# Context rows padded to 128, evidence blocks in one DMA each, weights in parts, and new orders around the guests of a four-layer attention kernel

## The reference

```python
def cross(xq, ctx):                       # layers 0, 2, 3; k, v of 1500 rows
    q, (k, v) = heads(xq @ Wq + bq), heads2(ctx @ Wkv + bkv)
    return softmax(q @ k.T / sqrt(8)) @ v
# layer 0
x = x + cross(ada(x), ada(ctx_1024)) @ Wp + bp
# layer 1, one head of 128
nx = layer_norm(x)
evidence = softmax((nx @ Wq) @ (ctx_1024 @ Wk).T / sqrt(128)) @ (ctx_1024 @ Wv)
c = concat(nx, evidence, cond)
routed = sum_e softmax(c @ router_W)[e] * (silu(c @ e_w1[e] + b1) @ e_w2[e] + b2)
x = x + sigmoid(silu(c @ gate_w1) @ gate_w2) * (routed @ out_w + out_b)
# layers 2 and 3
x = x + gate_a * self_attention(modulate(ln(x)))
x = x + cross(ln(x), ctx_1024)
x = x + gate_m * (gelu(modulate(ln(x)) @ W1 + b1) @ W2 + b2)
```

## Time and profile before

| | |
|---|---|
| median of 3 runs | 873.31 us (870.72 to 874.67) |
| the profiled execution | 873.29 us, its span 871.5 us |
| mean granted TensorE clock | 0.955 |
| busy: TensorE, VectorE, ScalarE, GpSimd | 780.7, 580.4, 514.1, 386.8 us |
| DMA | 106.55 MB, mean 122 GB/s |
| chain that ended last | TensorE 74%, DMA 9%, VectorE 6% |

### The profile page before, as it was taken

The page is one execution under the profiler, slowest core; times in us unless marked ns, Lnnn a source line. Parts: engine busy times, 40 slices in busy tenths (PEclk is TensorE's granted clock), DMA queues, the critical chain, the costliest instruction groups (busy, mean ns, idle before and its releaser), DMA issues.

```text
span 871.5 us, 23503 instructions
## 1 busy us (share of the span) xinstructions
PE 780.7 (90%) x9735; PEld 548.0 (63%) x9735; DVE 580.4 (67%) x1344; ACT 514.1 (59%) x826; POOL 386.8 (44%) x540
## 2 busy tenths in 40 slices
PE   6659999997699899967889999899999989999986
PEld 4227667765466576546657776666667666666664
DVE  7945778673288477722873777766778847777824
ACT  8435767665155567642654778565766646777552
POOL 8754767753017277620261775525332514333000
PEclk9797999999799999989996999999999989999999
DMA  8695545835614246443250553441643423543100
GB/s 216 174 245 146 151 132 171 236 92 168 168 28 127 74 108 170 131 143 110 84 155 13 144 140 90 127 127 52 174 131 98 142 74 104 162 131 101 37 3 11
DMA packets 87230, 106.55 MB, mean 122 GB/s; under 512 B 13278, under 2 KB 79838, under 8 KB 86868
## 3 DMA queue, kind: packets, MB, share of 16 engines
q1 hardware_dynamic: 83092, 103.04, 42.9%
q10 hardware_dynamic: 4032, 2.00, 0.9%
HBM read 41.17 MB, written 0.23 MB: 48 GB/s over the span
## 4 chain that ended last, share of the span: by engine, by line
PE 74%; DMA 9%; DVE 6%; ACT 4%; POOL 4%; issue 2%; SPq 1%; POOLq 0%; ACTq 0%
PE oacc_ps L692 14%; PE ring_ps L667 14%; PE score_ps L681 12%; PE ring_ps L644 7%; PE ring_ps L651 7%; DMA tok<-ctx_nat 6%; DVE max_sb L785 3%; PE ring_ps L636 2%; PE ring_ps L1042 2%; PE ring_ps L1596 2%; DMA kstack<-part_sb 2%; PE ring_ps L657 1%; POOL kstack L2103 1%; ACT prob_sb L764 1%; PE ring_ps L1072 1%
## 5 line engine op out<-in xcount | busy, mean ns | idle before, releaser
L785 DVE TENSOR_REDUCE max_sb<-ring_ps 128x1 f32<-128x500 f32 x576 | 368.8, 673 | 122.2 <-PE ring_ps L667 120.3
L764 ACT ACTIVATE prob_sb<-score_ps 125x896 f32<-125x896 f32 x288 | 256.6, 922 | 93.8 <-PE score_ps L681 91.1
L860 POOL TENSOR_TENSOR key_sb<-key_sb,part_sb 128x500 f32<-128x500 f32 x72 | 82.4, 1144 | 318.7 <-ACT key_sb L746 318.4
L667 PE MATMUL ring_ps<-kstack,qstack 128*128 128x500 bf16 x576 | 200.0, 386 | 18.5 <-DMA kstack<-part_sb 11.8
L681 PEld LDWEIGHTS score_ps<-qstack,kstack 128*128 128x128 bf16 (+1 forms) x2304 | 141.9, 103 | 39.6 <-issue 10.8
L681 PE MATMUL score_ps<-qstack,kstack 128*128 128x112 bf16 (+1 forms) x2304 | 160.3, 216 | 1.8 <-ACT prob_sb L764 1.0
L692 PE MATMUL oacc_ps<-prob_sb,val_sb 125*32 125x168 f32 (+1 forms) x3456 | 141.6, 297 | 0.5 <-ACT prob_sb L764 0.5
L692 PEld LDWEIGHTS oacc_ps<-prob_sb,val_sb 125*32 125x32 f32 x3456 | 98.4, 110 | 49.2 <-issue 21.9
L667 PEld LDWEIGHTS ring_ps<-kstack,qstack 128*128 128x128 bf16 x576 | 52.1, 99 | 79.5 <-issue 28.4
L865 POOL TENSOR_TENSOR part_sb<-key_sb,part_sb 128x500 bf16<-128x500 f32 x72 | 82.2, 1142 | 5.1
L851 POOL TENSOR_SCALAR hat_sb<-nat_sb,norm_now 125x128 f32<-125x128 f32 x184 | 80.3, 453 | 1.4
(11 more groups left out here) (266 smaller groups left out, 984.2 us busy)
## 6 DMA issues: line engine op xcount, KB each, us to landing
kstack<-part_sb SPq DMA_DIRECT2D x432, 125.0 KB, 2.4
nat_sb<-ctx_nat SPq DMA_DIRECT2D x16, 672.0 KB
qstack<-qpart_sb SPq DMA_DIRECT2D x60, 112.0 KB, 2.3
nat_sb<-ctx_T SPq DMA_DIRECT2D x8, 750.0 KB, 4.7
ev_in<-ctx_T SPq DMA_DIRECT2D x16, 250.0 KB
ev_in<-ctx_nat SPq DMA_DIRECT2D x16, 250.0 KB
w_sb<-ctx_nat SPq DMA_DIRECT2D x5, 672.0 KB
w_sb<-weights SPq DMA_DIRECT2D x1, 3076.5 KB, 10.9
```

The lines of the kernel that those rows point to most:

```text
L667: last = pe.matmul(ps[:, 0:KB], queries(p, n, D), kstack[:, u, p, j * KB:(j + 1) * KB], start=True, stop=True)
L764: return act.activation(dst, score_ps[0:CK, c % 2, :, 0:HALF], ACT.Exp)
L785: return dve.tensor_reduce(max_sb[:, p, j:j + 1], ring_ps[:, self.bank[f"{i}.{name}"], 0:KB], AX.X, ALU.max)
L860: return pool.tensor_tensor(rest, rest, part_sb[:, 0, cols], ALU.subtract)
```

## The change

1. `ctx_nat` is padded to 128 rows, and a context comes in one DMA (it was 112 rows and 13 rows).
2. A new array `ctx_blocks` holds the evidence blocks as 128 rows x 2 x 512, one DMA each.
3. The weights of layers 1 and 2 come in four parts, one at the start of each of the periods 0 to 3, each behind a count of finished statistics. The modulation weights move from the startup to period 1. Contexts 5, 6 and 7 are loaded for their statistics at the starts of periods 0, 1 and 2, context 4 behind item 0's keys; its statistics move from VectorE's startup to period 0.
4. Only the first half batch's queries are stacked ahead of item 0's keys; the other six DMAs go behind them.
5. The second half of `kstack` is cleared behind item 0's hats and gets its ones behind item 0's values.
6. TensorE: V0 to V2 of period -1 stand ahead of MTa, K2 behind MTb; period 0 begins with S0 and S1.
7. mods goes from period 0, anch from period 3, to period 4 behind S9.
8. The tables are written anew. e0a's and e0b's heads run further in periods 4 and 8 (w, l, g2, o0 to o2 at their ends); e2b's own scores go from period 18 to the end of 17; e3a's proj goes from period 22 to 20 and its u0 and u1 from 24 to 23. A table LATE gives periods 7 and 11 an order of their own on TensorE and VectorE, in which the maxima (of items 8 and 12) stand further behind the scores.

```diff
-            sp.dma_start(to[0:NAT_SPLIT, :, :], ctx_nat[n, 0:NAT_SPLIT]).then_inc(loaded, 16)
-            sp.dma_start(to[NAT_SPLIT:CK, :, :], ctx_nat[n, NAT_SPLIT:CK]).then_inc(loaded, 16)
+            sp.dma_start(to, ctx_nat[n]).then_inc(loaded, 16)
...
+                order = LATE[eng, p].split() if (eng, p) in LATE else order
+                if eng == "pe" and p == 0:
+                    order = ["S0", "S1", *[n for n in order if n not in ("S0", "S1")]]
...
-                    for t in range(2):
-                        n = HB * self.h + 2 * k + t
-                        if kind == 0:
-                            sp.dma_start(block[:, t, 0:KB], ctx_T[n][:, i * KB:(i + 1) * KB]).then_inc(into, 16)
-                        else:
-                            sp.dma_start(block[0:CK, t, :].rearrange("p (c k) -> p c k", c=4), ctx_nat[n][:, 4 * i:4 * i + 4, :])\
-                                .then_inc(into, 16)
+                    sp.dma_start(block, ctx_blocks[2 * self.h + k, NJ * kind + i]).then_inc(into, 16)
...
-            stack_queries(sp, queries_ready(d0), a0.qstacked, (0, 1))
+            stack_queries(sp, queries_ready(d0), a0.qstacked, (0, 1), (0,))
             sp.wait_ge(keys_cleared, 1)
...
-            for n in range(STATS_FIRST, 7):
-                load_context(sp, stats_buffer(n), n, stats_loaded[n])
-            w0, w1 = W_AT["L2_W_mod"][0], W_AT["L1_Wq"][0]
-            sp.dma_start(w_sb[:, w0:w1], weights[:, w0:w1]).then_inc(loaded_wm, 16)
-            sp.wait_ge(stats_done, STATS_AT[2] + 1)
-            load_context(sp, stats_buffer(7), 7, stats_loaded[7])
+            stack_queries(sp, queries_ready(d0), later_queries, halves=(1,))
+            load_context(sp, stats_buffer(4), 4, stats_loaded[4])
             sp.wait_ge(keys_cleared, 2)
-            for p in a0.periods(-1):
+            a0.run("sp", sp, -1)
+            for p in a0.periods():
+                if p < 4:
+                    sp.wait_ge(stats_done, p + 3)
+                if p < 3:
+                    load_context(sp, stats_buffer(p + 5), p + 5, stats_loaded[p + 5])
+                if p == 1:
+                    w0, w1 = W_AT["L2_W_mod"][0], W_AT["L1_Wq"][0]
+                    sp.dma_start(w_sb[:, w0:w1], weights[:, w0:w1]).then_inc(loaded_wm, 16)
+                if p < 4:
+                    w0, w1 = weights_slot((0, 1, 3, 2)[p])
...
+                    sp.dma_start(w_sb[:, w0:w1], weights[:, w0:w1]).then_inc(loaded_w1, 16)
                 a0.run("sp", sp, p)
...
-            for u in range(2):
-                pool.memset(kstack[:, u, :, :].bitcast(F32), 0.0).then_inc(buffers_ready, 1)
-            pool.wait_ge(buffers_ready, 2)
+            pool.memset(kstack[:, 0, :, :].bitcast(F32), 0.0).then_inc(buffers_ready, 1)
+            pool.wait_ge(buffers_ready, 1)
...
+            a0.run("pool", pool, -2, beside=lambda name, p: name == "hat2" and
+                   pool.memset(kstack[:, 1, :, :].bitcast(F32), 0.0).then_inc(buffers_ready, 1))
+            for p in a0.periods(-1):
```

More of the change, by code:

```diff
@@ L109 @@
 VALUES = 3
-NAT_DMAS = 32
-NAT_SPLIT = 112
+NAT_DMAS = 16
 class Ticks:
@@ L294, in pixart_program @@
-def pixart_program(nc, ctx_nat, ctx_T, x_T, cond_T, weights, vectors, identity, out):
+ 'pre': {('dve', 4): 'mods:M2.1 scales:M2.1 gates:M2.1 twice:M2.1 anch:M2.1',
+         ('pe', 4): 'mods:S9 anch:S9',
+         ('pool', 5): 'keys0:hat2 keys1:hat2 pads0:hat2 pads1:hat2 ones:hat2'}}
+BANKS = {0: '01201201201210210210212012012012102',
+ 1: '1021021020120102012010210210210210210',
+ 2: '2102102012021021021020120120120120120',
+ 3: '1201201021012012012010210210210210210',
+ 4: '21021020120102102120120120120102102100210212012011212010210210211012012',
+ 5: '102101201201210120121201200202020200210210210201',
+ 6: '2012102101010202102102012012102102010210210210210210',
+ 7: '2102102102102012102102101201201201201',
+ 8: '201201210210120210201201201021010210221020102102101202120120122102210',
+ 9: '210212012012102102012012010210210212101011021020',
+ 10: '1021021021010120201201021021201201020120120120120120',
+ 11: '1201210210210210210120120120120120202',
+ 12: '0210210120121021021201201202102102102102101201',
+ 13: '2012012101201212122202102102012012010210210210210101202',
+ 14: '012012101021212012012012012012012012012',
+ 15: '0120102021212012012012012012012012',
+ 16: '0120102020101201201201201201021201201201202',
+ 17: '1201210201020120120101010210210210212012012012121202',
+ 18: '012012102021212012012012012012012012012',
+ 19: '0120102021212012012012012012012012',
+ 20: '01201020212120120120120120120120120',
+ 21: '1201210102020120120120120120120120',
+ 22: '1201201201201201201201201201',
+ 23: '2012012',
+ 24: '0120120120'}
@@ L295, in pixart_program @@
+def pixart_program(nc, ctx_nat, ctx_T, ctx_blocks, x_T, cond_T, weights, vectors, identity, out):
     ctx = ExitStack()
@@ L447, in stack_queries @@
                         rows = slot_rows(slot)
-                        for h in range(2):
+                        for h in halves:
                             sp.dma_start(half_queries(rows.start, rows.stop, h, rows.step),
@@ L1452, in sync @@
             def sync(self, sp):
-                w1 = W_AT["L1_Wq"][0]
-                sp.wait_ge(stats_kept, B)
-                sp.dma_start(w_sb[:, w1:W_L3], weights[:, w1:W_L3]).then_inc(loaded_w1, 16)
-                yield "w1"
-            sent = ["w1"]
+                return
+                yield
         class First(Half):
@@ L2108, in _ @@
             pool.memset(ev_q[:, HT:HT + 8], 0.0).then_inc(ev_pad, 1)
-            for p in a0.periods(-2):
+            a0.run("pool", pool, -2, beside=lambda name, p: name == "hat2" and
+                   pool.memset(kstack[:, 1, :, :].bitcast(F32), 0.0).then_inc(buffers_ready, 1))
+            for p in a0.periods(-1):
                 a0.run("pool", pool, p)
@@ L2159, in _ @@
                 .then_inc(queries_cleared, 1)
-            for u in range(2):
-                act.wait_ge(buffers_ready, u + 1)
-                fill(key_stack(u)[SHIFT_ROW:SHIFT_ROW + 2, :], bf16_ones[:, :], 1.0).then_inc(keys_cleared, 1)
+            act.wait_ge(buffers_ready, 1)
+            fill(key_stack(0)[SHIFT_ROW:SHIFT_ROW + 2, :], bf16_ones[:, :], 1.0).then_inc(keys_cleared, 1)
             act.wait_ge(d.dve.sem, d.dve.after("scales0"))
@@ L2264 @@
     nat = a["ctx_1024"].reshape(B, CK, NC, D)
+    rows = np.zeros((B, D, NC, D), nat.dtype)
+    rows[:, 0:CK] = nat
+    flat = nat.transpose(0, 3, 2, 1).reshape(B, D, NJ, KB).transpose(0, 2, 1, 3)
+    ctx_blocks = np.zeros((B // 2, 2 * NJ, D, 2, 4 * D), nat.dtype)
+    for t in range(2):
+        ctx_blocks[:, 0:NJ, :, t, 0:KB] = flat[t::2]
+        ctx_blocks[:, NJ:, 0:CK, t] = nat[t::2].reshape(B // 2, CK, NJ, 4 * D).transpose(0, 2, 1, 3)
     a["L1_WkT"] = a["L1_Wk"].T
@@ L2276 @@
     arrays = {
-        "ctx_nat": nat,
+        "ctx_nat": rows,
         "ctx_T": nat.transpose(0, 3, 2, 1).reshape(B, D, S),
+        "ctx_blocks": ctx_blocks,
         "x_T": a["x"].reshape(NT, D).T,
```

77 lines of the change are left out of this document (29 added, 48 removed), and 197 rows, old and new, of tables (EARLY_L0, GUESTS, LATE).

## The result

The changed kernel takes 836.68 us (median of 4 runs, 835.44 to 841.14), the kernel before 873.99 on the same chips: a ratio of 0.958 with an interval from 0.953 to 0.963, 37 us less. Here and in the experiments a time is the median of all runs, and a ratio leaves out those that took over 1.5% longer than the fastest of the same kernel. The forecast was 825 and a range of 807 to 847. The profiled execution took 835.44 us with a span of 833.6, so 37.9 of the forecast 47.9 us are there, and 10 are to be found.

What follows compares the result with a forecast made beforehand. TensorE bounds the kernel, with transfer waits and the low clock behind them. −16 − 2.3 − 10.4 − 15.7 − 3.5 = −47.9 us on a span of 871.5 gives 823.6, plus 1.8 beside the span: 825; range 807 to 847.

Steps and rivals of the forecast that it cites:

- Periods 4 to 6: e0a's stretch: block waits and low clock go, −15.5; anch and mods move into period 4, 2.3 and 2.8; sum −10.4 us.
- I leave 2.5 us of idle time: e0a's stretch: idle time kept for sums waiting on probabilities and first blocks on free slots, giving 24.2 us.
- Periods 8 to 10: e0b's stretch falls from 35.80 to 23.1 us, −12.7; half of period 10's low-clock loss goes, −3; sum −15.7 us.
- Periods 7 and 11: Maxima placed behind scores; together with periods 12 to 18 put at 0 ± 4 us.
- the same instructions on a full TensorE: Reason given for 0 ± 4 us in periods 7, 11 and 12 to 18, with maxima behind scores and e2b's head moved.
- Startup: Up to the end of period 0: −8.4 − 5.0 − 3.7 + 1.1 = −16 us, bounds −4 and −20.
- the scores no longer stand behind M0.0: Startup: S0 begins at about 56.5 instead of 64.91, no longer behind item 1's M0.0; −8.4 us.
- Periods 0 to 3: anch leaves the end of period 3, −2.3 us; added weights, context and block DMAs costed at nothing.
- the rival of the held SP: Periods 0 to 3: SP waits for statistics counts, with loads ahead of the stacks; four times 15 us lost, 885; chance 0.04.
- Tail: e3a's u0 and u1 move into period 23, only y stays behind the last values; −3.5 us.
- the one on other waits in the block stretches: Sums wait for late ScalarE or VectorE; a third to two thirds of 28 us kept, 835 to 844; chance 0.13.
- The first rival: Startup's wait only moves: item 1's column still lands late, M0.0 waits behind S1; −5 instead of −16, 836; chance 0.12.

Runs made afterwards that it cites:

- natural blocks of 125 rows: The changed kernel with natural evidence blocks loaded as 125 rows in one DMA each, turned blocks still 128 rows: 863.20 us, ratio 0.985.
- shift row first: The changed kernel with SP sending e0a's shift row ahead of the context load in period 6: 831.44 us, ratio 0.948.
- the kernel of the three edits: The changed kernel with both kstack memsets first, e0a's shift row ahead of the context load, and the template's order in periods 7 and 11: 820.85 us, ratio 0.940.

## Why the forecast was right in direction and 12 us too low

**What bounds it** was right: TensorE, and on it the waits for transfers with the low clock behind them.

**Blocks** were the change's main part, as the sum had it. The 125 rows were the cause of the low rate (natural blocks of 125 rows, 23 to 26.5 us), and on the kernel before the blocks alone give 16.5 and 11.1 us in the two stretches, against 15.5 and 12.7 in the sum.

**Periods 4 to 6** are where the sum failed most: -3.5 instead of -10.4. The step that failed is "I leave 2.5 us of idle time": I looked for the next wait inside e0a's stretch, behind probabilities and slots, and that was right there (period 4 has 2.9 us of idle time). But the new table lets e0a's head end in period 5, and its own scores now open period 6, ahead of item 6's scores and behind a shift row that SP issues after a context. The forecast saw that pattern in period 10 of the kernel before, took half of its cost off, and did not look for it in the new period 6; the order of SP and TensorE there would have told it. It cost 9.2 us (shift row first). The two moved products took 2.80 and 2.38 us, as priced; what the low clock behind them adds is open. With the shift row first the three periods come to 137.2 us, and to 134.3 in the kernel of the three edits, which is -11.7 against the forecast's -10.4.

**Periods 8 to 10** came out at -17.5 against -15.7; the blocks alone gave 11.1 of it, and the rest came with the other parts of the change, of which no run has the new tables alone. The trace shows what differs in period 10, where e0b's own scores no longer open the period but stand behind a step of scores and one of the turned context:

```profile
425.93 0.75 PE L1034 MATMUL ring_ps<-qstack,w_sb 128*128 128x112 bf16 x12 [1.88 <-DMA qstack<-own_shift]
```

They wait for the shift row as long as before (1.88 us, and 1.83 there), but no half clock follows at once; one of 3.4 us comes at 435.9, ten us later, where 13.7 us followed at once in the kernel before. So a wait of the same length had no stretch at half clock right behind it here; that the place in the order is the reason is not shown.

**Periods 7 and 11**, put at 0, cost 5.6. With the 2.5 that periods 12 to 18 gave, the line's total of +3.1 lies within its 4, but the reason given for it, "the same instructions on a full TensorE", failed: maxima behind the scores leave VectorE's reductions (0.67 us each) for the end of the period, and TensorE waits for them. LATE costs 4.6 of the 5.6. Why periods 12 to 18 became shorter no run shows.

**Startup**: -13.4 instead of -16, and two steps need mending. The rule of the Trainium skill that the forecast named ("SBUF — State Buffer", section "Who interferes with whom") agrees with this trace, 4.80 us against 0.39, but I priced it too low: I let the cast wait 3.5 us and cost nothing else. It waited 4.4, ScalarE's copies, which stand in a fixed order, carried it on to the key steps, and without it period 0 ends 3.4 us earlier. And "the scores no longer stand behind M0.0" was given the 8.4 us; the experiments give them to the bytes: with the loads out of the way the old order is as fast, and with the bytes back even the new order loses 3.5 us. What the new order would save with the bytes in place was not run.

**Periods 0 to 3**: -3.1 for -2.3. The parts, contexts and blocks cost nothing there: periods 1 to 3 moved 193 GB/s, and TensorE was busy for 73.68 of 75.30 us, so the rival of the held SP falls.

**Tail**: -5.3 in the last period and +1.8 ahead of it, -3.5 in all, as forecast. y went from 3.25 us to 1.75, since it no longer runs at half clock; the sum had taken its gain from waits alone. That the total is met to 0.1 us is in part luck: the wait shrank by 1.8 us instead of 2.7, the 1.5 us of y were not in the sum, and the price ahead of it was 1.8 instead of 1.

Of the rivals, none came true as a whole. The nearest was the one on other waits in the block stretches, with the right time (835 to 844) and the wrong cause: not ScalarE's probabilities but a DMA behind another in SP's queue. The first rival names 836 as well, by chance: item 1's M0.0 waited for no stack, and the startup lost 2.6 us of its gain, not 11.

## What to carry to other kernels

When a large wait is taken away, look at every place where the new order puts a short, dependent chain alone on the bounding engine, and follow its last transfer through the queue that issues it: here a row behind a 768 KB context cost 9.2 us, and turning two SP steps round won it back. A tile of 125 rows can move at two fifths of the rate of one of 128 (131 against 311 GB/s here), so padding gains although it adds bytes. A long clear that is moved out of the way of one engine must be checked against what runs beside it at its new place: 5.10 us of memset on GpSimd held a cast on VectorE for 4.80 us instead of 0.39.
